# Gate rows spread by DMA in the gated layer, and a last expert layer in two parts

## The reference

```python
x = x + _L0_xcond_ref(ctx, _layernorm(x), ...)      # windowed attention
x = x + _L0_ffn_ref(_layernorm(x), ...)             # gated experts: the "gated layer"
x = x + _L1_xcond_ref(...)                          # attention with 16 heads
x = x + _L1_ffn_ref(...)                            # 8 experts, 2 per token
x = x + _L2_xcond_ref(...); x = x + _L2_ffn_ref(...)
x = x + _L3_xcond_ref(...)
x = x + _L3_ffn_ref(...)                            # 8 experts, 1 per token: the "last layer"
```

```python
h = silu(xf @ w1e + b1e) * (xf @ w3e + b3e)
y = y + we[:, None] * (h @ w2e + b2e)               # for each expert e, we = cw[:, e]
z = silu(xf @ sw1 + sb1) * (xf @ sw3 + sb3) @ sw2 + sb2
```

```python
gates, idx = max(softmax(xt @ Wr + br)), argmax(...)
h = relu(xn @ W1[idx] + b1[idx]);  y = (h @ W2[idx] + b2[idx]) * gates
```

## Time and profile before

| | |
|---|---|
| median of 3 runs | 918.86 us (916.9 to 919.8) |
| profiled execution, first to last instruction (span) | 904.5 us |
| PE busy | 709.5 us (78%) |
| DVE busy | 471.9 us (52%) |
| ACT, POOL busy | 243.3 us, 248.6 us |
| mean granted TensorE clock | 0.857 of full speed |
| PE's share of the chain that ended last | 66% |

### The profile page before, as it was taken

How to read it: one execution, slowest core, us unless ns; L and a number is a source line. 1 busy time by engine, 2 the same in 40 slices (tenths; PEclk the granted TensorE clock), 3 DMA queues, 4 the chain that set the end, 5 groups by cost and what they waited for, 6 DMA issues and landing times.

```text
span 904.5 us, 13708 instructions
## 1 busy us (share of the span) xinstructions
PE 709.5 (78%) x4589; PEld 453.8 (50%) x4589; DVE 471.9 (52%) x1390; ACT 243.3 (27%) x377; POOL 248.6 (27%) x326
## 2 busy tenths in 40 slices
PE   4567999999999899784599838689877967529960
PEld 3553445444444545453499814244442757518950
DVE  6547785747656555567322135354337357663432
ACT  1112323232223333231144402123223722103310
POOL 4821010010204121535200064611130037860014
PEclk9657999999999999886799966689899996558995
DMA  9910000000001300001122110100000050002112
GB/s 360 417 52 1 0 1 1 0 1 0 1 0 33 155 2 1 24 19 35 59 71 72 51 38 21 34 2 1 1 1 1 2 186 1 19 31 64 43 42 84
DMA packets 25350, 43.58 MB, mean 48 GB/s; under 512 B 3265, under 2 KB 19393, under 8 KB 24130
## 3 DMA queue, kind: packets, MB, share of 16 engines
q1 hardware_dynamic: 22210, 36.41, 11.2%
q0 software_dynamic: 3072, 6.30, 2.4%
HBM read 26.05 MB, written 16.65 MB: 47 GB/s over the span
## 4 chain that ended last, share of the span: by engine, by line
PE 66%; DVE 15%; POOL 7%; issue 4%; DMA 3%; ACT 2%; SPq 1%; DVEq 0%; POOLq 0%; ACTq 0%
PE banks L338 62%; POOL SHARE L2113 2%; DVE mx L1400 2%; DVE stats L983 2%; PE banks L345 2%; DMA SHARE<-rows_out,slots 2%; POOL XN L2002 1%; POOL rstd L1995 1%; PE banks L768 1%; ACT XNT L1701 1%; POOL rows_in L2129 1%; DVE mv L988 1%; POOL SELECT L2057 1%; PE banks L895 1%; DVE X L999 1%
## 5 line engine op out<-in xcount | busy, mean ns | idle before, releaser
L1995 POOL TENSOR_TENSOR rstd<-veps,neghalf 128x4 f32<-128x4 f32 x32 | 33.1, 1035 | 390.9 <-DVE veps L991 390.8
L338 PE MATMUL banks<-XNT,SLOT 128*128 128x512 f32 x256 | 124.8, 611 | 4.1 <-DVE cw L1261 4.1
L338 PE MATMUL banks<-U 128*128 128x128 f32 (+3 forms) x816 | 123.2, 387 | 1.8 <-ACT U L1868 0.9
L2113 POOL DMA_INDIRECT SHARE<-rows_out,slots x48 | 46.0, 958 | 165.3 <-DMA rows_out<-SHARE 151.7
L1762 ACT ACTIVATE SHARE<-banks,SM 128x512 f32<-128x512 f32 x68 | 46.7, 687 | 154.0 <-PE banks L338 153.9
L338 PEld LDWEIGHTS banks<-U 128*128 128x128 f32 (+3 forms) x816 | 82.4, 182 | 10.5 <-issue 7.7
L1400 DVE TENSOR_REDUCE mx<-banks 128x8 f32<-128x616 f32 x64 | 51.2, 800 | 66.7 <-PE banks L338 65.6
L1284 DVE SCALAR_TENSOR_TENSOR SHARE<-banks,SM,SHARE 128x512 f32<-128x512 f32 x68 | 51.0, 750 | 62.9 <-PE banks L338 59.7
L338 PEld LDWEIGHTS banks<-XNT,SLOT 128*128 128x128 f32 x256 | 50.0, 196 | 67.5 <-issue 67.2
L1802 ACT ACTIVATE U<-banks 103x1536 f32<-103x1536 f32 x32 | 46.4, 1450 | 81.7 <-PE banks L338 81.7
L338 PE MATMUL banks<-SHARE,SLOT 128*128 128x512 f32 x128 | 66.9, 603 | 0.0
(11 more groups left out here) (298 smaller groups left out, 1157.5 us busy)
## 6 DMA issues: line engine op xcount, KB each, us to landing
rows_in<-U SPq DMA_DIRECT2D x1, 8192.0 KB, 33.4
SLOT<-l1w SPq DMA_DIRECT2D x2, 2048.0 KB, 22.2
SLOT<-f SPq DMA_DIRECT2D x2, 2048.0 KB, 10.1
U<-rows_in SPq DMA_DIRECT2D x64, 64.0 KB, 1.8
SLOT<-l3w SPq DMA_DIRECT2D x2, 2048.0 KB, 8.5
rows_out<-SHARE SPq DMA_DIRECT2D x14, 256.0 KB, 2.3
SLOT<-w SPq DMA_DIRECT2D x1, 2048.0 KB, 13.5
SM<-small SPq DMA_DIRECT2D x1, 1376.5 KB, 9.1
```

The source lines that it names most:

```text
L338: return nc.tensor.matmul(out_, lhsT, rhs, start=start, stop=stop, **kw)
L1995: power = g.tensor_tensor(rstd[:, a, :], veps[:, a, :], neghalf[:], ALU.pow)
L2113: g.indirect_dma_start(YG[:, j % RING, :], None, ys[0:BLOCKS[l] * P, :], bass.IndirectOffsetOnAxis(ap=slots[:, t, k:k + 1].bitcast(u32), a ...
```

## The change

**Gated layer.** `pairsel`, `cw3` and the `G` matmuls are gone. When DVE has copied a chunk's turned gates to `cwT`, SP stores them to a DRAM tensor of 32 x 512 and waits for that store. Then it loads each pair's two rows back, each on 64 partitions, into a ring `GR` of 8 buffers (`SLOT[3]`). The load of row pair n waits until pair n - 8 has been used. DVE multiplies `T1` by the ring's buffer. `A` and `C` have three banks each, the shared expert is step 0, and the bias product comes after step 8. The layer's first `up` comes ahead of `gatesT(0)`. The down weights of layer 3, which had been loaded to `SLOT[3]` at the start, are loaded after the gated layer.

**Last layer.** Chunks 0 and 1 are part 0, chunks 2 and 3 part 1. Each part has its own row tensors (`rows_in2`, `rows_out2`; the zero store gets 4 MB more) and 8 + 7 = 15 blocks in groups of 4, 4, 4 and 3, so there are 30 blocks. Part 0 is placed as soon as chunk 1 is routed. Chunk 3's routing and the placing of part 1 stand between the blocks of part 0. Part 0's gathers may run under the blocks of part 1.

```diff
-                for i in range(1, BATCH + (3 if ahead else 1)):
+                for i in range(1, BATCH + 1):
...
-                    if i < PAIRS:
-                        mm(claim(pe, 4 + b, ("G", c, i))[:], pairsel[:, i, :], cw3[:, c % 2, :])\
-                            .then_inc(bank_full[4 + b], 1)
...
+                def up(c, k):
 
                     xc = XNT[:, chunk(c)]
+                    i = k - 1
+                    w1 = SLOT[0][:, i * P:(i + 1) * P] if k else small("sw1")
+                    w3 = SLOT[0][:, 2048 + i * P:2048 + (i + 1) * P] if k else small("sw3")
+                    r = (c * STEPS + k) % 3
+                    mm(claim(pe, A_BANKS[r], ("A", c, k))[:], w1, xc).then_inc(bank_full[A_BANKS[r]], 1)
+                    mm(claim(pe, C_BANKS[r], ("C", c, k))[:], w3, xc).then_inc(bank_full[C_BANKS[r]], 1)
+
+                def down(c, k):
+                    if k == 0:
+                        claim(pe, 6, ("oT", c))
+                        drained(pe, ("C", c, 0))
+                    else:
+                        pe.wait_ge(sem("h_ready"), c * PAIRS + k)
...
                 for c in range(BATCH):
-                    drained(pe, ("cwT", s, c))
-                    pe.wait_ge(sem("cw3_ready"), c + 1)
...
+                    for k in range(STEPS):
+                        if c == 0 and k == 1:
+                            gatesT(0)
+                            pe.wait_ge(sem("w13_loaded"), 16)
+                        up(c, k)
...
+                logits, count = routing(s, 3) if l == 3 else (None, None)
...
                 busy(BUSY_LOAD)
                 rows_in(0)
+                if l == 3:
+                    prep_xt(4 * s + BATCH - 1)
+                    logits(BATCH - 1)
...
+                        if c == 1:
+                            for step in range(PLACE_STEPS):
+                                place(0, step)
+                            place_tokens(0)
...
+                    row = c * PAIRS + k - 1
+                    dve.wait_ge(sem(f"gate_rows{row % SPREAD_RING}"), 16 * (row // SPREAD_RING + 1))
+                    mark(v.tensor_tensor(h, T1, GR[:, row % SPREAD_RING, :], ALU.mult), "h_ready")
...
+                relu(0)
+                route(last)
+                for step in range(4):
+                    choose(last, step)
+                relu(1)
+                choose(last, 4)
+                relu(2)
+                finish(last)
+                for b in range(3, BLOCKS[l]):
+                    if PLACE_FROM <= b < PLACE_FROM + PLACE_STEPS:
+                        place(1, b - PLACE_FROM)
+                    if b == PLACE_FROM + PLACE_STEPS:
+                        place_tokens(1)
+                    relu(b)
+                    if COMBINE_FROM <= b < COMBINE_FROM + 2 * TPC:
+                        c, k = divmod(b - COMBINE_FROM, TPC)
+                        combine(s, l, c, k)
...
-            mark(g.memset(pairsel[:], 0.0))
-            for k in range(3):
-                m = pairsel[32 * k:32 * k + 32, :, :].rearrange("p i (h f) -> p i h f", h=2)
-                mark(g.affine_select(out=m, in_=m, compare_op=ALU.not_equal, fill=1.0, base=0,
-                                     pattern=[[-2, PAIRS], [-1, 2], [0, F0]], channel_multiplier=1))
...
-            sp.dma_start(SLOT[3][:], l1w2_in).then_inc(sem("down_loaded1"), 16)
...
+            def gate_rows(s, c):
+
+                drained(sp, ("cwT", s, c))
+                sp.dma_start(gates_dram[c], cwT[:, c % 2, :]).then_inc(sem("gates_stored"), 16)
+                sp.wait_ge(sem("gates_stored"), 16 * (c + 1))
+                for i in range(PAIRS):
+                    n = c * PAIRS + i
+                    if n >= SPREAD_RING:
+                        sp.wait_ge(sem("h_ready"), n - SPREAD_RING + 1)
+                    sp.dma_start(GR[:, n % SPREAD_RING, :],
+                                 gates_dram[c][2 * i:2 * i + 2, :].unsqueeze(1).to_broadcast([2, F0, SEQ]))\
+                        .then_inc(sem(f"gate_rows{n % SPREAD_RING}"), 16)
...
+                late = 1 if PARTS[l] > 1 else 0
+                for g in range(4):
                     load(g)
...
+                    if g >= late and g + 4 - late < len(groups):
+                        load(g + 4 - late)
```

More of the change, by code:

```diff
@@ L265, in build @@
         b2row = SLOT[1][0:1, 0:E1 * D]
+        GR = SLOT[3][:].rearrange("p (r n) -> p r n", r=SPREAD_RING)
+        gates_dram = [nc.dram_tensor(f"gates{c}", (E0, SEQ), f32).ap() for c in range(BATCH)]
         xs = nc.dram_tensor("rows_in", (E1 * REGION, D), f32).ap()
@@ L326, in scaled_rows, with place_of, inner_downs, rows_count @@
             return sem(f"ln_scaled{n // BATCH}"), TPC * (n % BATCH + 1)
+        def place_of(l, b):
+            g = max(g for g, (first, _) in enumerate(BLOCK_GROUPS[l]) if first <= b)
+            first, n = BLOCK_GROUPS[l][g]
+            return g, b - first, b - first == n - 1
+        def inner_downs(l, b):
+            return done_before[l] + sum(not place_of(l, n)[2] for n in range(b + 1))
+        def rows_count(l, g):
+            return 16 * sum(n for i, (_, n) in enumerate(BLOCK_GROUPS[l]) if i <= g and i % 4 == g % 4)
         def group_of(c, k):
@@ L1141, in window_layer @@
                     mark(v.memset(carry[:], 0.0))
-                for i in range(BATCH + (2 if ahead else 1)):
+                if ahead:
+                    place, place_tokens = placing(s + 1, 3)
+                for i in range(BATCH + 1):
                     c = i - 2
@@ L1172, in window_layer @@
                 if gated_next:
-                    for step in range(SPLIT_STEPS):
-                        split(0, step)
+                    split(0)
             def gates(s):
@@ L1594, in up_weight @@
                         .then_inc(sem(f"up_copied{s}"), 1)
-                place()
                 if l == 1:
+                    for step in range(PLACE_STEPS):
+                        place(0, step)
                     for b in range(UP_RING):
@@ L1601, in topk_layer @@
                         heads_prep(key)
-                place_tokens()
-                for b in range(BLOCKS[l]):
-                    if l == 1:
-                        if b >= UP_RING:
-                            up_weight(b)
-                    else:
-                        relu(b)
+                    place_tokens(0)
+                    for b in range(UP_RING, BLOCKS[l]):
+                        up_weight(b)
+                    return
+                norms, route, choose, finish = routing(s, 3)
+                last = BATCH - 1
+                relu(0)
[15 more added lines that the diff above has]
+                        combine(s, l, c, k)
             def choice_layer(s):
@@ L1684, in _ @@
             if layers[-1][0] == TOPK:
[L1685 removed]
+                for c in range(BATCH // 2, BATCH):
                     combine(len(layers) - 1, layers[-1][1], c)
@@ L1729, in window_layer @@
                 exps(0)
-                for i in range(1, BATCH + (2 if ahead else 1)):
+                for i in range(1, BATCH + 1):
                     c = i - 2
@@ L2196, in load @@
                 def load(g):
+                    first, n = groups[g]
+                    rows = part_ready(g // per_part) if g % per_part == 0 else None
+                    if g == 0 and l == 1:
+                        full(sp, VALUE_PREPS[2][-1])
                     if g >= 4:
                         full(sp, ("XB", s, g - 4))
-                    for j in range(4):
-                        row = first_row(g, j) if g else first_rows[j]
-                        sp.dma_start(XB[:, g % 4, j, :], xs[bass.ds(row, P), :])\
+                    for j in range(n):
+                        row = rows[j] if rows else first_row(first + j)
+                        sp.dma_start(XB[:, g % 4, j, :], XS[l][g // per_part][bass.ds(row, P), :])\
```

387 lines of the change are left out of this document (208 added, 179 removed).

## The result

| | before | changed |
|---|---|---|
| median of 4 runs | 918.75 us | 1061.24 us (1046.57 to 1066.16) |
| span of the profiled execution | 904.5 us | 1055.2 us |
| ratio, 95% interval | | 1.1505 [1.1396, 1.1615] |

What follows compares the result with a forecast made beforehand. PE alone was taken to bound the gated layer, then the row loads. Span 904.5 + 138.4 (gated layer) - 8.8 (start) - 1.6 (last layer) = 1032.5, with 14.4 around it 1047 us; range 885 to 1080, likeliest case 1010 to 1080.

Steps and rivals of the forecast that it cites:

- The engines of a row load: Gated layer: 2 of 16 DMA engines carry each gate-row load, chance 0.80 at 5.0 to 5.6 us a row.
- The rival with 16 engines: Gated layer: sixteen engines carry a row load in 0.7 us, PE sets the pace, 893.3 us in all; chance 0.13.
- 5.3 us a row: Gated layer: time of one row load on two engines, taken between 5.04 us by bytes and 5.55 by packets.
- First row: Gated layer: first row lands at 81.4 us on before's clock, from issue at 74.8, latency 1.3 and transfer 5.3.
- Boundaries: Gated layer: at three chunk boundaries the next loads wait 3.8 us for the gates' store, together 11.4 us.
- The start: Start of the kernel: without `pairsel` POOL comes to the next rows earlier, -8.8 us.
- Two engines hide PE's gains: Gated layer: the terms of PE's work, such as 14.1 us leaving PE, are hidden under the row loads.
- The last layer: Last layer in two parts: starts 11.5 us earlier, blocks end 8.4 us later, gathers give back 10.0; sum -1.6 us.
- late row load: Last layer: loads of group 4 and later go out one group later, so a row load is late by 1.8 us.
- +6 if DVE is late for relu: Last layer: upper bound of +6 us if chunk 3's routing makes DVE late for `relu`, against -1.6.
- What lies around the span: Whole kernel: 14.4 us added to every span, as the profiled execution spans 904.5 and the median is 918.86.
- two engines at 3.0 us a row: Gated layer rival: an engine alone moves 128 KB in 3.0 us or less, time about 905; chance 0.02.

Runs made afterwards that it cites:

- e1: Changed kernel with each row load cut in two, one gate row to its 64 partitions each, source outermost dimension 64 instead of 2: 913.44 us, ratio 0.985.
- e6: As e1, with the source of each one-row load written as 4 x 16 x 512, outermost dimension 4: 951.27 us in one execution.
- e5: Changed kernel with each row load writing only columns 0 to 255, half the bytes in as many packets: 946.96 us in one execution.
- e2: Kernel before with the gated layer of e1 alone, the last layer as it was: 893.03 us, ratio 0.970.
- e11: e2 once more, unchanged: 900.21 us, ratio 0.980.
- e12: e3 with DVE's eight additions of part 0 moved from between the relus to after the last relu: 917.96 us, ratio 1.009 to the kernel before.
- e3: Kernel before with the last layer in two parts alone: 925.26 us, ratio 1.007.
- e10: Kernel before once more, unchanged, for a second trace: a single execution of 919.64 us.
- e7: e2 with the three 2 MB weight loads held back until the next layer's first scatter: 912.91 us, ratio 0.985 to the kernel before.
- e8: Kernel before with a third 2 MB weight load behind the gated layer: 926.01 us, ratio 1.002.

## Why the prediction was right, and where its terms were off

**The engines of a row load.** Right: two, by packets (130), by rate (50 GB/s), and by e1 and e6, which differ from each other in the outermost dimension and in nothing else. The rival with 16 engines was the e1 kernel; its gated layer is what that rival described.

**5.3 us a row.** 5.20 measured. The byte bound of 5.04 was nearer than the packet bound of 5.55, and e5 says why: it is the bytes that decide. 63 x 0.1 = 6.3 us too many.

**First row.** 72.26 us on the changed kernel's clock; the forecast's 81.4 less the 8.8 of the start is 72.6. Its parts were off by a little each: the gates were copied earlier (61.57 + 0.68, not 63.8), the store took 2.2 us, and the load 7.7 and not 6.6.

**Boundaries.** Predicted 3 x 3.8 = 11.4 us. Over the boundary above, two periods took 249.56 - 236.58 = 12.98 in place of 10.40: 2.6 us. All 63 periods took 408.22 - 72.26 = 335.96, 8.4 us more than 63 x 5.20. The store was issued earlier than the forecast had it and waited in the engines' queues, so that SP's issue and part of the latency were already paid.

Together: the forecast for the gated layer's end was +138.4 - 8.8 = +129.6 us, measured +119.4.

**The start.** Right:

```profile
41.57 1.09 PE L371 MATMUL banks<-ident,XN 128*128 128x128 f32 x4 [1.89 <-POOL XN L2085]
```

50.40 in the earlier trace rows, 8.83 us earlier.

**Two engines hide PE's gains.** Right, and e2 shows that they are real once uncovered: its gated layer ended at 263.44 and e11's at 261.57, 26.1 and 27.9 us before the old one's end (predicted -24.0). The last two gate multiplications stand 2.57 us apart in both, as forecast, and 2.79 in before.

**The last layer.** The term that failed: predicted -1.6 us, measured +6.9. On a clock that starts at the first scatter, PE's first `up` comes at 29.65 us and before at 42.97, 13.3 us earlier (predicted 11.5), and 8 gathers follow the blocks, as said. But the blocks ended 17 us later and not 8.4:

```profile
948.72 1.64 PE L364 MATMUL banks<-U 128*128 128x128 f32 x10
...
950.10 1.13 DVE L1633 TENSOR_SCALAR SHARE<-banks,SM 128x128 f32<-128x128 f32 x4 [6.68 <-PE banks L364]
...
979.14 1.13 DVE L1633 TENSOR_SCALAR SHARE<-banks,SM 128x128 f32<-128x128 f32 x4 [0.86 <-DVE slots L1617]
...
994.24 1.13 DVE L1633 TENSOR_SCALAR SHARE<-banks,SM 128x128 f32<-128x128 f32 x4 [0.96 <-PE banks L364]
...
996.10 0.63 PE L793 MATMUL banks<-ident,U 128*128 128x128 f32 x4 [2.31 <-DMA U<-rows_in]
...
1004.96 1.13 DVE L1633 TENSOR_SCALAR SHARE<-banks,SM 128x128 f32<-128x128 f32 x4 [4.21 <-PE banks L364]
...
1034.47 0.36 SPq L2320 DMA_DIRECT2D rows_out<-SHARE  x1
...
1037.38 0.94 POOL L2192 DMA_INDIRECT SHARE<-rows_out,slots  x1 [26.31 <-DMA rows_out<-SHARE]
```

The relus of blocks 0 and 9 stand 29.0 us apart; nine blocks at the pace of a group of 4 (9.26 us) are 20.8. These are the blocks between whose relus DVE routes chunk 3 and places part 1. I had put 0.8 us there, and it is 8.2: each relu waits its turn on DVE, and `down` waits for it. In before, the same ten relus lie 20.08 us apart with 10.14 us of work on DVE; here DVE does 18.71 us of work, so 8.6 us of work more cost 9.0. This is read from the trace; no run moves the routing or the placing alone. The late row load was 2.31 us of waiting (predicted 1.8), but PE's granted clock then fell, to 0.50 from 999 to 1003 us: the two blocks behind the wait took 10.7 us (994.24 to 1004.96), and two such blocks without a wait 5.1, so it cost 5.6. The additions between relus, which I had put at nothing, make each of eight blocks 0.4 us longer (e12 against e3). The "+6 if DVE is late for relu" bound was the one to take.

**What lies around the span.** I took 14.4 us from 918.86 - 904.5. e10 shows 1.7 us around, and that the first trace came from an execution with a better clock in the layers between. In the sum the slip does no harm, as it comes to adding the change, 138.4 - 8.8 - 1.6 = +128.0 us, to the median of before. That +128.0 lies so near the 126.3 us that the two changed layers measured is luck: the gated layer was 10.2 us too many and the last one 8.5 too few. The medians moved by 142.5, and the 16 us between lie in layers that the change doesn't touch. From span to span the forecast was 1032.5 against 1055.2, 22.7 us short, and of these -10.2 are the gated layer, +8.5 the last, +24.4 the layers between.

Two sums of the forecast are a little off, and neither bears on the result: its lower bound of 1012 is 1014 by its own terms (1019 + 1.6 - 7), and two engines at 3.0 us a row come to 900 us and not 905.

**The clock behind the gated layer** is what stays open. I named a falling clock only for the gated layer, where it costs nothing, and not for the full layer behind it. The stretch took 80.97 to 83.81 us in the five traces with the old gated layer, and 99 to 108 us in eight of nine with the new one; the ninth is e11. PE's waiting (e1, e2), the loads (e7, e8) and the number of engines (e1) aren't the cause by themselves. In both kinds the attention layer begins with the same short lulls of PE. At one of them PE is busy 3.02 of 4 us in e11 (277 to 281 us) and in e2 (279 to 283), and the clock stays at 1.00 in the one and falls to 0.50 in the other. With the old gated layer it fell there too in e3 and e12, but was back within some 8 us, at a cost of 2.8 us. If both kinds of kernel had the same chance of a slow stretch and the executions were independent, all eight would be among the nine new ones in 9 of 3003 cases. So chance alone is unlikely, but no run shows what in the new gated layer does it, and the cause stays open. The medians fit an effect in most executions of the changed kernel: +119.4 + 6.9 = 126.3 from the two layers, 142.5 and 145.7 measured. But the layers further on differ by as much from trace to trace, so they don't prove it.

## What to carry to other kernels

Read the number of DMA engines from the small packets of a transfer, and before making a load that copies one row to many partitions, look at the outermost dimension of both of its access patterns: if it is 2, the load moves at the rate of two engines. Here, loads of one row each with 64 outermost used all 16 and gave back 142 us, for an edit of a few lines. A stage that PE fills completely gives back all that leaves PE, but takes in full any resource that is slower than PE's pace. In a stage where the second engine is half busy, work put between its short steps can still cost its full length (8.6 us of DVE's work cost 9.0, an addition of 0.35 us cost 0.4), because PE waits for each step and not for the sum.

## What the runs showed of the hardware that I had not expected

- A small store that spreads over all engines waits for the busiest: 64 KB took 2.2 us to land with free engines, and 13.7 us (222.90 to about 236.6) behind the last three row loads on two of them, at 5.2 us a load.
- SP's issue of a load takes longer when the queues are full: the first two took 0.5 to 0.6 us, the median of all 64 was 5.1 us on two engines, as long as a transfer, and 0.6 us with sixteen.
- Executions of one program differ by how often the clock falls in layers with short lulls. One and the same attention layer took 81 or 100 us, at a mean grant of 1.00 or 0.78, and the layers ahead of the last one, with the same work, 254 to 277 us (before and e7), at 0.83 to 0.74 (the two levels are 1.2 and 2.4 GHz). A single span is therefore known to no better than some 20 us here, however exact its rows are.
